# Turning x and the last layer's weights by VectorE in 32x32 blocks, spreading bias rows and condition by DMA

## What is computed

```
x is (4, 512, 256) float32, cond_8 is (4, 8); four residual layers, each conditioned per batch:
x = x + L0(x)   two of 8 experts (top 2 of softmax(cond)) and a shared one, each down(gelu(gate x) * (up x)), width 1024
x = x + L1(x)   one expert (argmax of cond), down(silu(up x + bu) * (gate x + bg)) + bd, width 512
x = x + L2(x)   x @ (sum_g cond[g] * weight[g] * mask).T + bias
x = x + L3(x)   x @ W_base.T + b_base + 2 * sum_e cond[e] * (x @ As[e].T) @ Bs[e].T
```

## Time and profile before

| | |
|---|---|
| median of three runs | 504.8 us |
| profiled execution, span first to last instruction | 503.2 us |
| TensorE busy | 495.4 us, 98% |
| VectorE busy | 344.5 us, 68% |
| ScalarE busy | 250.9 us, 50% |
| GpSimd busy | 19.8 us, 4% |
| DMA | 49.17 MB, mean 98 GB/s |

### The profile page before, as it was taken

How to read it: one execution, slowest core, us unless ns; L and a number is a source line. 1 busy time by engine, 2 the same in 40 slices (tenths; PEclk the granted TensorE clock), 3 DMA queues, 4 the chain that set the end, 5 groups by cost and what they waited for, 6 DMA issues and landing times.

```text
span 503.2 us, 7511 instructions
## 1 busy us (share of the span) xinstructions
PE 495.4 (98%) x2326; PEld 412.5 (82%) x2326; DVE 344.5 (68%) x566; ACT 250.9 (50%) x389; POOL 19.8 (4%) x36
## 2 busy tenths in 40 slices
PE   6999999999999999999999999999999999999997
PEld 5688688888888888888888888888888888888897
DVE  4657688985643767996653657888564376799666
ACT  4454444654554445564543644465454444556452
POOL 6003000000000020000000020000000002000000
PEclk9899999999999999999999999999999999999999
DMA  7848654139430233225732033213943023420001
GB/s 202 289 125 232 161 128 100 51 94 194 100 117 1 63 106 119 70 64 147 126 102 63 0 111 119 80 45 99 188 109 104 0 63 105 124 64 0 0 2 43
DMA packets 102995, 49.17 MB, mean 98 GB/s; under 512 B 53596, under 2 KB 101216, under 8 KB 102976
## 3 DMA queue, kind: packets, MB, share of 16 engines
q1 hardware_dynamic: 101200, 44.32, 32.8%
q0 software_dynamic: 1776, 4.62, 3.1%
HBM read 46.82 MB, written 2.10 MB: 97 GB/s over the span
## 4 chain that ended last, share of the span: by engine, by line
PE 96%; DMA 2%; SPq 1%; ACT 0%; issue 0%; DVE 0%; DVEq 0%
PE bank_a L940 10%; PE bank_a L941 10%; PE bank_a L942 10%; PE bank_b L942 10%; PE bank_b L941 10%; PE bank_b L940 10%; PE out L958 9%; PE out L962 9%; PE out L959 9%; DMA raw<-in_L_cond_shared_down 2%; PE tail L940 1%; PE tail L942 1%; PE tail L941 1%; PE tail L962 1%; PE tail L958 1%; PE tail L959 1%
## 5 line engine op out<-in xcount | busy, mean ns | idle before, releaser
L468 ACT ACTIVATE hid_hi<-hid 128x512 fp32r<-128x512 f32 x108 | 68.3, 632 | 105.2 <-DVE hid L587 63.0
L463 ACT ACTIVATE hid<-bank_a 128x512 f32<-128x512 f32 x96 | 57.3, 597 | 91.1 <-PE bank_a L942 91.1
L576 DVE TENSOR_TENSOR w_lo<-raw,w_hi 128x768 fp32r<-128x768 f32 x88 | 83.5, 949 | 3.3 <-ACT w_hi L455 3.3
L594 DVE TENSOR_TENSOR hid_lo<-hid,hid_hi 128x512 fp32r<-128x512 f32 x108 | 74.1, 686 | 14.0 <-ACT hid_hi L468 14.0
L587 DVE SCALAR_TENSOR_TENSOR hid<-bank_b,mine,hid 128x512 f32<-128x512 f32 x64 | 48.1, 751 | 46.7 <-PE bank_b L942 46.2
L455 ACT ACTIVATE w_hi<-raw 128x768 fp32r<-128x768 f32 x88 | 73.7, 838 | 3.1 <-DMA raw<-in_L_cond_shared_down 3.1
L940 PE MATMUL bank_a<-x_hi,w_hi 128*128 (+1 forms) x176 | 68.6, 390 | 0.0
L941 PE MATMUL bank_a<-x_lo,w_hi 128*128 (+1 forms) x176 | 68.6, 390 | 0.0
L942 PE MATMUL bank_a<-x_hi,w_lo 128*128 (+1 forms) x176 | 68.5, 389 | 0.0
L942 PE MATMUL bank_b<-x_hi,w_lo 128*128 (+1 forms) x176 | 68.5, 389 | 0.0
L940 PE MATMUL bank_b<-x_hi,w_hi 128*128 (+1 forms) x176 | 68.5, 389 | 0.0
(11 more groups left out here) (249 smaller groups left out, 711.0 us busy)
## 6 DMA issues: line engine op xcount, KB each, us to landing
raw<-in_L_cond_skill_gate SPq DMA_DIRECT2D x32, 256.0 KB, 2.9
raw<-in_L_cond_skill_up SPq DMA_DIRECT2D x32, 256.0 KB, 3.1
raw<-in_L_cond_skill_down SPq DMA_DIRECT2D x64, 128.0 KB, 3.2
raw<-in_L_cond_shared_down SPq DMA_DIRECT2D x26, 128.0 KB, 3.8
raw<-in_L_cond_shared_gate SPq DMA_DIRECT2D x12, 256.0 KB, 3.3
raw<-in_L_cond_shared_up SPq DMA_DIRECT2D x12, 256.0 KB, 3.5
early<-in_L_cond_weight POOLq DMA_DIRECT2D x2, 1024.0 KB, 8.9
raw_gate<-in_L_cond_W_gate SPq DMA_DIRECT2D x16, 128.0 KB, 3.1
```

Source lines behind the costliest of these rows:

```text
L463: nc.scalar.activation(hid[:, n % 2], bank_a[n % 2][:, :], func, **kw).then_inc(act_ready, 1)
L468: nc.scalar.activation(hid_hi[:, n % 2], hid[:, n % 2], ACT.Copy).then_inc(hid_hi_ready, 1)
L576: nc.vector.tensor_tensor(lo, raw[:, raw_slot(i // 2), :, (i % 2) * P:(i % 2 + 1) * P], hi.bitcast(F32), ALU.subtract).then_inc(split_lo, 1)
L594: nc.vector.tensor_tensor(hid_lo[:, n % 2], hid[:, n % 2], hid_hi[:, n % 2].bitcast(F32), ALU.subtract).then_inc(hid_lo_ready, 1)
```

## The change

TensorE keeps of the preparations x of batch 0, the spread of the routing and the bias products. x of batches 1 to 3 is loaded by four DMAs per batch in pieces of 128 bytes so that one VectorE transpose of 128x1024 in 32x32 blocks gives the layout wanted (`x_turn_blocks`, after steps 2, 3 and 5); ScalarE's high part is one instruction (`later_x_hi`, steps 3, 4, 6) and VectorE's low part too (`later_x_lo`, steps 4, 5, 8). W_base and Bs arrive in such pieces by 4 and 8 DMAs of GpSimd and are turned by two VectorE transposes in step 6 (`l3_turn_blocks`). The condition is spread by 8 small DMAs into `y_rows`; the matrices `expand`, `cond_t`, `bias_diag` fall away. The rest of `turn`'s VectorE work (y_lora, base_t plus the unit matrix, u3, bias2_m) follows in `l3_turn_blocks`, and TensorE's bias products wait for it (`l3_turn`). The bias rows go to DRAM and come back spread over the partitions. On SP, piece 3 now stands before x of batches 1 to 3. For the turned x, rows stand in the order (q p) instead of (p q): x of batch 0 is read, and all outputs are written, in runs of 1 KB per row instead of 2 or 4 KB.

```diff
-PREP_AT = {2: ("route",), 3: ("x", 1), 4: ("x", 2), 5: ("x", 3), 6: ("turn",), 8: ("bias",), 9: ("rows",)}
+PREP_AT = {2: "route", 8: "bias"}
+X_TURN_AT = {2: 1, 3: 2, 5: 3}
+X_HI_AT = {3: 1, 4: 2, 6: 3}
+X_LO_AT = {4: 1, 5: 2, 8: 3}
+L3_TURN_AT = 6
...
             # SP
-            x_rows = t["x"].rearrange("b (p q) d -> b p q d", q=NQ)
+            x_rows = t["x"].rearrange("b (q p) d -> b p q d", q=NQ)
+            def load_x(b):
+                blocks = t["x"][b].rearrange("(n j) (k q i) -> q j k n i", j=32, q=4, i=32)
+                for q in range(4):
+                    sp.dma_start(early[32 * q:32 * (q + 1), b * NQ * D:(b + 1) * NQ * D]
+                                 .rearrange("j (k n i) -> j k n i", k=KD, i=32), blocks[q]).then_inc(x_in[b], 16)
...
+            load_piece(3, splits_done(0, 1), *shared)
             for b in range(1, B):
-                sp.dma_start(x_nat[:, b], x_rows[b]).then_inc(x_in[b], 16)
-            load_piece(3, splits_done(0, 1), *shared)
+                load_x(b)
...
             # POOL
+            for q in range(4):
+                pool.dma_start(base_raw[rows].rearrange("j (k n i) -> j k n i", k=KD, i=32), base_blocks[q])\
+                for e in range(2):
+                    pool.dma_start(b3_raw[rows].rearrange("j (n e r) -> j n e r", e=2, r=R)[:, :, e, :], b3_blocks[q, e])\
+            for e in range(E):
+                pool.dma_start(y_rows[e * R:(e + 1) * R, :],
+                               t["cond_8"][:, e:e + 1].rearrange("b e -> e b").broadcast_to([R, B]),
...
-            pool.wait_ge(tail_ready, PREPS.index(("x", B - 1)) + 1)
+            pool.wait_ge(tail_ready, PREPS.index("x") + 1)
+            pool.wait_ge(x_turn, B - 1)
...
+            pool.wait_ge(bias_row_ready, 1)
+            pool.dma_start(bias_dram, bias_row[:, :]).then_inc(bias_rows_out, 16)
+            pool.wait_ge(bias_rows_out, 16)
+            pool.dma_start(bias_all[:, :, :].rearrange("p b d -> p (b d)"),
+                           bias_dram.rearrange("(a b) d -> a (b d)", a=1).broadcast_to([P, B * D])).then_inc(bias_rows_in, 16)
...
             # ACT
+            def later_x_hi(b):
+                act.wait_ge(x_turn, b)
+                nc.scalar.activation(x_hi[:, :, b * S:(b + 1) * S], x_turned[b].rearrange("p (k s) -> p k s", k=KD), ACT.Copy)\
...
             # DVE
+            def x_turn_blocks(b):
+                dve.wait_ge(x_in[b], 64)
+                nc.vector.transpose(x_turned[b], early[:, b * NQ * D:(b + 1) * NQ * D]).then_inc(x_turn, 1)
+            def later_x_lo(b):
+                dve.wait_ge(x_turn, b)
+                dve.wait_ge(x_hi_ready, KD + b)
+                nc.vector.tensor_tensor(x_lo[:, :, cols], x_turned[b].rearrange("p (k s) -> p k s", k=KD),
+                                        x_hi[:, :, cols].bitcast(F32), ALU.subtract).then_inc(x_lo_ready, 1)
+            def l3_turn_blocks():
+                dve.wait_ge(turn_in, 192)
+                nc.vector.transpose(base_t[:, :, :].rearrange("p k d -> p (k d)"), base_raw).then_inc(l3_turn, 1)
+                nc.vector.transpose(b3_t[:, :], b3_raw).then_inc(l3_turn, 1)
+                dve.wait_ge(y_in, 16 * E)
...
             # PE, prep
-                elif what[0] == "turn":
...
-                elif what[0] == "rows":
...
                 else:
+                    pe.wait_ge(l3_turn, 3)
```

More of the change, by code:

```diff
@@ L217, in build @@
         mine = sb("mine", [P, PICK])
+        bias_dram = nc.dram_tensor("bias_rows", (B, D), F32, kind="Internal").ap()
         bank_a = [ctx.enter_context(nc.psum_tensor(f"bank_a{n}", [P, S], F32)) for n in range(2)]
@@ L470, in prep_hi @@
             def prep_hi(what):
[L471 to L476, removed]
+                if what == "bias":
                     act.wait_ge(l3_in, 48)
@@ L533, in batch @@
                         prep_hi(PREP_AT[i])
+                    if first(b) and i in X_HI_AT:
+                        later_x_hi(X_HI_AT[i])
                     if with_tail:
@@ L770, in prep @@
             def prep(what):
[L771 to L780, removed]
+                dve.wait_ge(tail_ready, PREPS.index(what) + 1)
+                if what == "route":
                     sums = tail[:, 0, 0:B * PICK]
@@ L784, in prep @@
                         .then_inc(chosen_ready, 1)
[L785 to L803 removed]
+                    ins = nc.vector.tensor_copy(picks[:, :, :].rearrange("p b n -> p (b n)"), sums)
                 else:
                     dve.wait_ge(rows_moved, 16)
[L806 to L809 removed]
+                    nc.vector.tensor_tensor(bias_row[:, :], tail[0:B, 0, 0:D], bias3_b[:, :], ALU.add)\
+                        .then_inc(bias_row_ready, 1)
                     dve.wait_ge(l3_hi, 1)
@@ L812, in prep @@
                 ins.then_inc(tail_free, 1)
+            def x_turn_blocks(b):
[4 more added lines that the diff above has]
+                dve.wait_ge(x_hi_ready, KD + b)
+                cols = slice(b * S, (b + 1) * S)
+                nc.vector.tensor_tensor(x_lo[:, :, cols], x_turned[b].rearrange("p (k s) -> p k s", k=KD),
[5 more added lines that the diff above has]
+                dve.wait_ge(y_in, 16 * E)
+                chain(nc.vector.tensor_scalar(y_lora[:, :], y_rows[:, :], LORA_SCALE, None, ALU.mult))
+                dve.wait_ge(l3_turn, 2)
+                for k in range(KD):
+                    block_k = base_t[:, k, k * P:(k + 1) * P]
+                    nc.vector.tensor_tensor(block_k, block_k, ident[:, :], ALU.add)
+                dve.wait_ge(l3_in, 48)
+                chain(nc.vector.tensor_tensor_reduce(out=u3_work, in0=a3, in1=bias2_rows, scale=1.0,
+                                                     scalar=0.0, op0=ALU.mult, op1=ALU.add, accum_out=u3[:, :]))
+                nc.vector.tensor_scalar(u3_y[:, :], y_lora[:, :], u3[:, 0:1], None, ALU.mult)
+                nc.vector.tensor_copy(bias2_m[:, :, :], bias2[:, :].unsqueeze(2).broadcast_to([P, KD, B]))\
+                    .then_inc(l3_turn, 1)
             def l3_operand():
@@ L875, in batch @@
                         prep(PREP_AT[i])
+                        if PREP_AT[i] == "route":
+                            dve.wait_ge(tail_free, PREPS.index("route") + 1)
+                            stage_mine(0)
+                    if first(b) and i in X_LO_AT:
+                        later_x_lo(X_LO_AT[i])
+                    if first(b) and i in X_TURN_AT:
+                        x_turn_blocks(X_TURN_AT[i])
+                    if first(b) and i == L3_TURN_AT:
+                        l3_turn_blocks()
                     if first(b) and i == L3_OPERAND_AT:
@@ L1143, in prep @@
                 one = lambda out, lhs, rhs: nc.tensor.matmul(out, lhs, rhs, start=True, stop=True)
[L1144 to L1147, removed]
+                if what == "x":
                     for k in range(KD):
[L1149 to L1150 removed]
+                        pe.wait_ge(x0_in[k], 16)
                         for q in range(NQ):
[L1152 removed]
+                            ins = nc.tensor.transpose(tail[:, k, q * P:(q + 1) * P], x_nat[:, 0, q, k * P:(k + 1) * P],
                                                       ident[:, :])
[L1154 removed]
+                        if k == 0:
                             ins.then_inc(x0_turned, 1)
[L1156 removed]
+                elif what == "route":
                     pe.wait_ge(route_step, ROUTE_STEPS)
[L1158 to L1162, removed]
[L1163 to L1172 removed]
+                    ins = one(tail[:, 0, 0:B * PICK], ones[:, :], pick_diag[:, :, :].rearrange("p b n -> p (b n)"))
                 else:
+                    pe.wait_ge(l3_turn, 3)
                     rows = tail[0:B, 0, 0:D]
```

62 lines of the change are left out of this document (29 added, 33 removed).

## The result

The changed kernel takes 496.12 us in the median of four runs (495.62 to 496.42) beside 504.56 us; the ratio is 0.9826, interval 0.9807 to 0.9845. Three executions of the kernel before took 834, 1009 and 1766 us; the ratios and intervals leave them out, the medians count them.

The account below looks back on a forecast made before the run. TensorE was taken to bound the kernel (96% of the chain), with DMA setting the time before 18 us. Span 503.2 - 6.15 + 0.1 = 497.15, plus 1.6 gives 498.7 us; 8-in-10 range 497.1 to 501.3.

Parts of the forecast that it names:

- The sum's large terms: Preparations leaving TensorE in steps 2 to 6 and 9: 6.15 us gained, of which transposes 2.74 and bias rows 2.14.
- the start: Before 18 us, loads shared with GpSimd's queue: balance near nothing, bounds -0.8 and +1.5 us, taken as 0.
- the bound of -0.8 us: Before 18 us: the most that the changed loads were expected to gain at the start.
- The low end of the forecast: Whole time: 497.2 us, from 498.7 with +-1 us run to run and -0.8 from the start.
- The 1.6 us of the sum: Whole kernel: median of the runs stands 1.6 us above the profiled span, added to 497.15 to give 498.7.
- x in small pieces: Loads of x in 128-byte pieces at 152 GB/s: batch 1 through at 24.5 us, batch 2 at 28; no cost.
- starts with no idle time: Step 2: VectorE's 128x1024 transpose starts without idle time behind a DMA of x, at about 25 us.
- VectorE: Steps 3 to 7: added 128x1024 transposes of 1.2 us each; step 5 too full, 4.6 us against 4.08, lateness hidden.
- The slack of 2.45 us: Hand-over to TensorE: `hid_hi` is ready 2.45 us before its matmul wants it, so 1 us of lateness costs nothing.
- GpSimd's small pieces crowding the start: Rival, before 18 us: small pieces make weight piece 1 land 1.5 us later, 500.2 us; chance 0.08.

Follow-up runs that it names:

- a_transposes: Changed kernel with 8 idle transposes of the unit matrix put back on TensorE in each of steps 3, 4 and 5; 499.58 us beside 505.21.
- a_rows: Changed kernel with two idle 4x512 products by ones put back on TensorE in step 9; 498.93 us beside 505.21.
- b_again: Kernel before, unedited, run again for a second profile of its start; 504.96 us, ratio 0.9999.
- a_again: Changed kernel, unedited, run again in a second set of runs; 495.74 us beside 504.73.
- a_pool_first: Changed kernel with GpSimd's five larger loads issued first and the small pieces behind them; 501.43 us beside 504.86, ratio 0.9936.
- a_x_late: Changed kernel with SyncE waiting for the routing before it loads x of batches 1 to 3; 499.05 us beside 505.21.
- a_x0_pq: Changed kernel with x of batch 0 read in the old row order (p q); 495.74 us beside 504.86.
- a_pool_all_late: Changed kernel with all of GpSimd's loads held back behind the first activation; 494.88 us beside 505.21, ratio 0.9802.

## Why the prediction was off: point by point

**The sum's large terms** are right. TensorE's 6.15 us came as foretold, and a_transposes and a_rows give two of them back at 2.71 (2.74 foretold) and 2.14. From step 2 to the end the kernel lost 6.0 to 6.1 us, 6.05 by the sum.

**The failed step is "the start"**: "the balance is near nothing, bounds -0.8 and +1.5 us; I take 0". It gained 2.4 us in the profile. Three things were wrong in it. It weighed the loads over the whole stretch before 18 us, but the stretch that counts ends where piece 1 lands; I had written myself that the loads behind the small issues leave some 10 us later (8.2 measured), and then set 1.3 us of them against 1.5 us of dearer small pieces as if both shared the same time. Measured from 3 to 14 us, GpSimd's queue went from 26.0 to 15.6% of the engines, 1.1 us of all of them, and SyncE's from 66.6 to 85.4%. That is less than half of the 2.4 us: from 13 to 15 us the engines had, in the profile of the kernel before, a share of 0.71 and 0.78 while piece 1 was still under way. That GpSimd's loads delay piece 1 is shown by holding them back and putting them first; in what way they cost more than their share stays open. Second, the bound of -0.8 us was TensorE's idle time in front of the second half of step 1 (0.80 us; the prediction calls it step 0's), read in one profile in which the half clock stretched the matmuls of step 1 up to that point; at full clock (the profile after, and b_again) they end 1.7 us earlier and the whole lateness of the data shows. Third, one execution was taken for the start: piece 1 landed at 16.4 us in one profile of the kernel before and at 15.4 in the other. The low end of the forecast doesn't follow from its own terms either: 498.7 - 1 - 0.8 is 496.9, not 497.2; the time lies below that too.

**The clock** had no term. From the first set of runs (24), the average cost of its falls is 15/24 x 1.56 = 1.0 us per run of the kernel before, and none in the nine runs of the changed one. Full-clock runs against each other give 504.03 - 496.07 (the mean of the changed kernel's four) = 8.0 us, and 503.96 - 495.68 = 8.3 beside a_again. So 8.4 to 9.0 is about 6.1 of matmuls, some 2 of the start and what lies around, and some 0.3 to 1.0 of clock. The start and the clock are not separated more finely, since a fall in the start can cost nothing: in the kernel before's profile it slowed matmuls that then still had to wait for ScalarE, behind piece 1. That the unsplit products and transposes bring the falls is only suggested: putting them back brought falls in five of eight runs, and one profile has one 1.3 us behind the products. Against it, kernels without them fall too: all ten runs of a_pool_first, two of four of a_x_late, one of four each of a_x0_pq and a_pool_all_late. What makes the clock fall stays open.

**Around the span**, between it and the whole time, there is 1.64 us after and 1.85 before in the median, 1.6 to 1.7 in all runs of the one and 1.8 to 1.9 in all of the other: 0.2 us more that had no term. The 1.6 us of the sum was the median of the runs less the span of what must have been a slower execution than the median one, so it isn't what lies around the kernel before; that it fits the changed one is luck. The cause of the difference wasn't looked for.

**x in small pieces**: x of batch 1 was put at 24.5 us and is there at 24.6, batch 2 at 28, there at 28.6. SyncE's twelve issues took 14.7 us (9.1 plus 2 foretold); hidden, as said. The first VectorE transpose did wait for its data (1.92 us); "starts with no idle time" was wrong, and the slack took it.

**VectorE**: the transpose takes 1.24 us (1.2). In steps 5 to 7 it is busy 4.08, 4.08 and 4.01 us of 4.08, with no cost. The slack of 2.45 us is what it rests on, and a_x_late measured 2.6.

**The rivals**: GpSimd's small pieces crowding the start was the right place with the wrong sign, since I priced the pieces and not the order; a_pool_first shows such a crowded start when the order is the other one, at 5.3 us, a part of it clock, instead of the 1.5 foretold. By the rule of the Trainium skill (DMA: Bandwidth & Descriptors, Queues, rings and completion order) that queues are served in turn, GpSimd's packets delay SyncE's. The table above fits that: from 31.8% to 15% of share, step 2 starts 7 to 8 us earlier; no run shows the turns themselves.

## What to carry to other kernels

Where the start waits for loads, loads of another queue in that stretch can delay it, also those that nobody needs for 40 us. Look at each queue's share of the DMA engines up to the landing that releases the first work, and try to hold the others back by a wait; then look at what they meet where they now land, since here all of them held back began the steps 1.7 to 2.4 us earlier and the time shows no clear gain. When a change puts issues into a queue, ask what is now late behind them, since late can be a gain. Take a bound from a profile only after looking whether the clock was full there, and a start only from more than one profile. The hand-over slack between engines, read as when it is ready against when it is wanted, predicted here within 0.2 us what lateness costs.

## What had not been expected of the hardware

- The granted clock falls to half in the middle of gapless matmuls (b_again, 59.3 to 62.7 us). In 15 of 24 runs of the kernel before its mean is below 0.999, and these are 1.56 us longer than the others.
- Holding back 0.5 MB of GpSimd's loads makes the kernel before 1.7 us faster (0.8 to 2.7, b_pool_late), all 0.9 MB 2.7 us (1.8 to 3.6, b_all_late), though none of them is needed before step 6.
- Four loads of 128-byte pieces that take 3.04 us to issue in the kernel before take 1.23 us each when twelve follow each other (14.74 us for x), and four of the layer-1 weights took 5.54 us in the changed kernel.
